# Layer 0 attention: the squares' sums are dealt out by a transfer, the key bias is a column of the keys, and rounding and queries change engines

## The chip, the cores and the metric

One Trainium2 chip (trn2), and the program runs on one of its cores. The metric is the device time of one execution in microseconds (us); less is better. Engines are TensorE (PE; PEld its weight loads), VectorE (DVE), ScalarE (ACT), GpSimd (POOL) and SyncE (SP), which issues nearly all DMAs.

## The reference

Two layers of gated cross attention with a feed-forward part behind each. The change lies in layer 0's attention, of which this is what matters (B = 4 batches, S = 256 tokens, 1601 context positions, H = 256, 8 key groups of 2 heads, head size D = 128):

```python
q  = ln(fp8_linear(ln_out, wq))  * qln_w  + qln_b      # per head, over D
k  = ln(fp8_linear(ln_out, wk))  * kln_w  + kln_b
qx = ln(fp8_linear(ln_out, wqx)) * qxln_w + qxln_b
kx = ln(einsum(cond, w_kv_x)[k]) * kxln_w + kxln_b
core = softmax(q  @ k.T  / sqrt(D)) @ v                # 256 own keys
xout = softmax(qx @ kx.T / sqrt(D)) @ vx               # 1601 context keys
cat  = concatenate([core, xout])
catq = fp8(bf16(clip(cat / smooth, -448, 448)))
x = x + tanh(g) * (catq @ wproj.T) * scale
```

## The kernel before

The program is written engine by engine: each of `sp_attention`, `pool_attention`, `dve_attention`, `act_attention` and `pe_attention` is one loop with its steps in an order chosen by hand, and semaphores join them. An iteration `it` is one pair of batch and key group (NGB = 32 of them). In iteration `it` the engines compute the attention of pair `it` (four query tiles `n = 4*it ... 4*it+3` of 128 rows) and prepare keys, values and queries of pair `it + 1`. During iterations 0 to 11 the weights of later groups are split into bf16 high and low parts as well.

Every product in fp32 quality is made of bf16 parts: a tensor has a high part and a low part (the remainder), and three products (`THREE`) are added. Keys and queries are `KK` and `QT`, values `VV`, probabilities `PB`, which DMA transposes turn into `PT`.

*Keys.* TensorE makes the unnormed keys of a pair in four blocks of PSUM (`keys`). ScalarE writes the high part (`keys_high`) times the norm's weight, and the squares `sq`; VectorE writes the low part (`keys_low`). The norm's factor of each key is not put into the keys: it multiplies the scores. For it TensorE sums the squares over D against a tile of ones (`squares`, 468 columns into each of four rows' groups), ScalarE copies the sums to `sqs` (`sums_out`), four transposes put them on partitions (`turn_squares`), VectorE copies them with epsilon to `ssc` [117 x 16] (`squares_out`), POOL raises them to the power -1/2 (`key_norm`, `rr`), TensorE transposes `rr` (`turn_norms`), ScalarE copies it to `rsr` (`norms_out`), and SP writes 16 rows of 468 bytes to DRAM (`row_out`) and reads them back as one row for all 128 partitions (`row_in`; its target is `x` for even and `rsb` for odd pairs).

*Scores.* `scores(n, half)` makes 1024 and then 577 + 256 columns. `scaled(n, piece)` on VectorE multiplies the scores by the row of factors, writes them to `S32` and takes the maximum (`mxp`, `mx`). `offset(n)` forms `nmx = c - (mx + c)`, where `c` is the bias of the keys times the query, which shifts all scores of a row alike. `c` comes from eight products with one column (`kb`, in `values(it, 3)`), which ScalarE copies from PSUM to `cb`. Then ScalarE takes exponentials, VectorE inverts the sums (`invert`), ScalarE writes the high probabilities (`p_hi`), VectorE the low ones (`p_lo`), and POOL both for the 256 own keys (`split_self`). SP transposes them (`turn_p`), and `times_v` multiplies by the values.

*Queries.* `turn_queries` leaves transposed normed queries in PSUM; ScalarE writes the high part `QT` from it (`query_high`), VectorE the full one `t32` (`query_full`), POOL the difference (`query_low`).

*Rounding to fp8.* VectorE divides, clips and takes the exponent bits `ye` (`exponents`); POOL makes the number `ym` from them (`magnitudes`: at least 2^-6, times 1.5 * 2^20) and adds and takes it away again (`add_magnitudes`, `take_magnitudes`). Then `project` multiplies with `wpb`, the split projection weights; `wpr` holds them as loaded.

*What sets the order.* SP issues one DMA after the other, so a wait holds everything behind it. The blocks of `SLOTS` take the three PSUM banks `pa`, `tb0`, `tb1` in turn; `wait_bank` waits until the block three slots before is read. A half of a score waits for the scaling of the same half of the score before:

```python
if n:
    e.wait_ge(s["mm"], 3 * (n - 1) + (1, 3)[half])
```

Of the kernel before, what the change touches and what calls it, by code (L numbers as in the profile page):

```python
# [13 lines left out]
P = 128  # L14
# [14 lines left out]
KC = SC + S  # L29
KTILES = KT + TB  # L30
# [12 lines left out]
ROUND_F8 = 1.5 * 2.0 ** 20  # L43
ROUND_INT = 1.5 * 2.0 ** 23
# [13 lines left out]
DCOLS = ["qln_w", "qln_b", "qxln_w", "qxln_b", "kln_w", "kln_b", "kxln_w", "kxln_b"]  # L58
# [14 lines left out]
pa_full k_sq k_lo sums_out ssq_out kr_pow rst_out v_hi v_lo st_done mv_done rs_pow nm_done normed  # L73
q_hi q_t32 q_lo pw_in pw_last pw_hi pw_lo acc_done
bank_full mm maxed negmax exp_s sum_read p_pad p_hi p_lo s_hi s_lo
# [28 lines left out]
def build(nc, A, out):  # L104
    m = Mem()
    whole = ExitStack()
    with whole:
# [5 lines left out]
        m.rs_d = nc.dram_tensor("rs_d", (2, SQN, SQW), F32, kind="Internal").ap()  # L113
# [9 lines left out]
def allocate(nc, m, whole):  # L123
# [15 lines left out]
    m.kb = sb(whole, "kb", [P, 2], BF16)  # L139
# [12 lines left out]
    with ExitStack() as attn:  # L152
# [7 lines left out]
        with ExitStack() as c:  # L160
            sb(c, "free_start", [P, BEFORE], BF16)
            m.wf = [sb(c, "wf0", [P, IC, WCOLS], F32), None]
            sb(c, "free_keys", [P, 2 * 2 * NQ * P + 2 * KC - 2 * IC * WCOLS], BF16)
# [17 lines left out]
        with ExitStack() as c:  # L181
            m.stage = [sb(c, f"stage{i}", [P, STAGE], BF16) for i in range(2)]
            m.wsb = sb(c, "wsb", [P, 2 * IC * WCOLS], BF16)
            m.sq = sb(c, "sq", [P, RSC], F32)
            m.sqs = sb(c, "sqs", [P, SQT * SQW], F32)
# [4 lines left out]
            kk[0] = sb(c, "KK0", [P, 2, KC], BF16)  # L190
            vv[0] = sb(c, "VV0", [P, 2, KTILES, D], BF16)
            sb(c, "free_mid", [P, 256], F32)
            qt[1] = sb(c, "QT1", [P, 2, 2, NQ * P], BF16)
            kk[1] = sb(c, "KK1", [P, 2, KC], BF16)
# [13 lines left out]
            m.ssc = sb(c, "ssc", [P, SQN], F32)  # L208
            m.rr = sb(c, "rr", [P, 32], F32)
            m.rsr = sb(c, "rsr", [32, P], F32)  # L210
            m.cb = [sb(c, f"cb{i}", [P, 2 * NQ], F32) for i in range(2)]
            m.mxp = [sb(c, f"mxp{i}", [P, 1], F32) for i in range(2)]
            m.mx = [sb(c, f"mx{i}", [P, 2], F32) for i in range(2)]
            m.mxc = [sb(c, f"mxc{i}", [P, 2], F32) for i in range(2)]
# [5 lines left out]
            m.ym = sb(c, "ym", [P, 512], F32)  # L220
# [6 lines left out]
        with ExitStack() as c:  # L227
# [14 lines left out]
            m.wg = sb(c, "wg", [P, IC, NE], F32)  # L242
            m.brow = sb(c, "brow", [P, NE], F32)
# [304 lines left out]
def pool_prologue(e, m, s):  # L548
# [9 lines left out]
    e.memset(m.rr[:, :], 0.0).then_inc(s["p_pad"], 1)  # L558
    e.memset(m.sq[:, KC:RSC], 0.0).then_inc(s["p_pad"], 1)
# [235 lines left out]
def pe_prologue(e, m, s):  # L795
# [8 lines left out]
         ("V2",), ("RS", "V3"), ("PR",))  # L804
ORDER = tuple(w for slot in SLOTS for w in slot)
SLOT = {w: n for n, slot in enumerate(SLOTS) for w in slot}
RS0 = 392
LAG = 3

PAIRS = 2 * G  # L810
# [77 lines left out]
def wait_bank(e, s, it, what):  # L888
# [6 lines left out]
    if SLOTS[at] == ("PR",) and 0 <= it < LAG:  # L895
        at -= 3
# [1993 lines left out]
```

## Time and profile before

| what | value |
|---|---|
| time, median of 3 runs (lowest to highest) | 1789.63 us (1786.24 to 1790.2) |
| span of the profiled execution | 1787.7 us |
| time of that execution around its span | not shown on the page |
| PE busy | 1631.5 us (91%) |
| DVE busy | 1474.9 us (83%) |
| ACT busy | 1386.3 us (78%) |
| POOL busy | 1367.9 us (77%) |
| DMA queue q1 | 602960 packets, 258.57 MB, 70.1% of 16 engines |

A profile is one execution. Busy times of the engines overlap, so an engine's share says how full it is and not what the end depends on; that is read from gaps, waits and the distance from start to start. Ends of matmuls are modelled: of matmuls the starts are read. Instructions of a group run on in the next row's time by some hundredths.

### The profile page before, as it was taken

The page shows a single profiled execution, that of the slowest core. Times are in us where ns is not written, and L with a number is a line of the kernel's source. Part 1 is how long each engine was busy: PE and PEld are TensorE (multiplying, and loading weights), DVE is VectorE, ACT ScalarE, POOL GpSimd, SP SyncE. Part 2 cuts the span into 40 slices and gives each one's busy share as a digit, 9 for nine tenths or more (in the row PEclk, how much of TensorE's full clock was granted, in tenths as well). Part 3 has the DMA queues.
Part 4 walks back from the last instruction along what each step waited for, and adds up shares of the span by engine and source line. Part 5 has one row for each costly group of instructions (what it writes and reads, how often), then busy time and mean ns, then how long its engine had stood idle before and what let it go on. Part 6 is the DMA issues. An engine that isn't in the chain of part 4 may idle for free. (4 is left out here: it accounts for less than half of the span.)

```text
span 1787.7 us, 44278 instructions
## 1 busy us (share of the span) xinstructions
PE 1631.5 (91%) x16245; PEld 1038.3 (58%) x16438; DVE 1474.9 (83%) x3476; ACT 1386.3 (78%) x2365; POOL 1367.9 (77%) x1171
## 2 busy tenths in 40 slices
PE   3389999999999999999999999997898999999997
PEld 1256776777767767777777777765454333333332
DVE  8889999999999989999999999998896765645422
ACT  4287887888878777887887888775234999999996
POOL 3557787887878888888888888887897998979500
PEclk8599999999999999999999999999899999999999
DMA  4268999999899979999999999998523222222100
GB/s 168 93 130 180 184 187 193 198 194 190 189 199 184 200 150 198 191 231 184 195 195 192 217 213 190 194 186 160 171 42 110 41 44 75 43 37 43 31 14 13
DMA packets 603176, 261.42 MB, mean 146 GB/s; under 512 B 568784, under 2 KB 575952, under 8 KB 601552
## 3 DMA queue, kind: packets, MB, share of 16 engines
q1 hardware_dynamic: 602960, 258.57, 70.1%
q8 instruction: 131, 2.15, 0.5%
q14 instruction: 85, 0.70, 0.1%
HBM read 99.15 MB, written 17.28 MB: 65 GB/s over the span
## 5 line engine op out<-in xcount | busy, mean ns | idle before, releaser
L1800 PE MATMUL pv<-PT,VV 128*128 128x256 bf16 (+1 forms) x2880 | 340.9, 275 | 9.2 <-DMA PT<-PB 9.2
L1780 PE MATMUL score<-KK,QT 128*128 128x512 bf16 (+2 forms) x1795 | 315.6, 318 | 32.6 <-DVE mxp L1249 24.3
L2370 POOL TENSOR_TENSOR l_rr<-l_rr,mhalf 128x32 f32<-128x32 f32 (+1 forms) x60 | 332.8, 5546 | 5.0
L1521 ACT ACTIVATE PB<-S,rsum 128x1024 bf16<-128x1024 f32 (+1 forms) x256 | 246.2, 988 | 105.3 <-DVE rsum L1281 101.1
L1800 PEld LDWEIGHTS pv<-PT,VV 128*128 128x128 bf16 (+1 forms) x2880 | 280.7, 99 | 76.4 <-issue 35.2
L1272 DVE SCALAR_TENSOR_TENSOR PB<-S,rsum,PB 128x1024 bf16<-128x1024 f32 (+1 forms) x256 | 318.7, 1246 | 2.7 <-ACT PB L1521 2.6
L1780 PEld LDWEIGHTS score<-KK,QT 128*128 128x128 bf16 x1920 | 159.9, 98 | 164.5 <-DVE mxp L1249 32.3
L1511 ACT ACTIVATE S<-S,nmx 128x1601 f32<-128x1601 f32 x128 | 209.7, 1638 | 28.3 <-DVE nmx L1263 27.8
L2636 ACT ACTIVATE P<-score 128x1024 f32<-128x1024 f32 x196 | 199.4, 1063 | 12.7 <-PE score L2728 6.0
L1076 POOL TENSOR_SCALAR S<-S,rsum 128x256 f32<-128x256 f32 x128 | 122.0, 954 | 86.1 <-DVE rsum L1281 86.1
L2748 PE MATMUL pv<-P,V 128*9 128x256 f32 (+1 forms) x2288 | 153.9, 384 | 3.8 <-DVE pv L2174 2.4
L1637 PE MATMUL tb<-stage,wsb 128*128 128x512 bf16 x767 | 150.7, 340 | 4.9 <-DVE stage L625 4.1
L1088 POOL TENSOR_SCALAR ym<-ye 128x512 f32<-128x512 bf16 x64 | 139.9, 2186 | 11.5 <-POOL catq L1104 5.4
L1059 POOL TENSOR_TENSOR rr<-ssc,mhalf 117x16 f32<-117x16 f32 x32 | 92.8, 2899 | 49.0 <-DVE ssc L1215 49.0
L1249 DVE CUSTOM_DVE_ANT_0 S<-score,x 128x1024 f32<-128x1024 f32 (+1 forms) x128 | 104.4, 816 | 7.0 <-PE score L1780 3.2
L1461 ACT ACTIVATE kn<-pa,a_nm,a_rs 128x128 f32<-128x128 f32 x256 | 96.0, 457 | 18.3 <-POOL a_nm L1041 18.3
L1249 DVE CUSTOM_DVE_ANT_0 S<-score,rsb 128x1024 f32<-128x1024 f32 (+1 forms) x128 | 104.4, 815 | 5.7 <-PE score L1780 1.9
L1637 PEld LDWEIGHTS tb<-stage,wsb 128*128 128x128 bf16 x768 | 67.3, 99 | 71.6 <-issue 10.6
L1689 PE MATMUL tb<-wsb,stage 128*128 128x128 bf16 x1536 | 98.1, 221 | 4.4 <-DVE KK L1161 4.4
L2728 PE MATMUL score<-QB,KT 32*128 32x256 bf16 (+1 forms) x1110 | 93.5, 275 | 7.0 <-ACT P L2636 4.7
L1430 ACT ACTIVATE KK<-tb,dcols 128x512 bf16<-128x512 f32 (+1 forms) x128 | 76.0, 593 | 28.6 <-PE tb L1637 27.9
L1689 PEld LDWEIGHTS tb<-wsb,stage 128*128 128x128 bf16 x1536 | 92.7, 99 | 8.4 <-DVE KK L1161 6.9
(275 smaller groups left out, 3686.7 us busy)
## 6 DMA issues: line engine op xcount, KB each, us to landing
x<-rs_d SPq DMA_DIRECT2D x16, 936.0 KB, 7.6
rsb<-rs_d SPq DMA_DIRECT2D x16, 936.0 KB, 6.0
wsb<-w_split SPq DMA_DIRECT2D x46, 256.0 KB, 4.7
wsb<-w_split SPq DMA_DIRECT2D x23, 512.0 KB, 5.2
wpr<-in_wprojT SPq DMA_DIRECT2D x23, 512.0 KB, 3.9
context_d<-stage SPq DMA_DIRECT2D x16, 400.2 KB, 3.7
l_ctx<-context_d SPq DMA_DIRECT2D x4, 1601.0 KB, 8.1
rawh<-in_w_all SPq DMA_DIRECT2D x12, 512.0 KB, 5.6
```

What stands on the lines that cost most here:

```text
L1088: e.tensor_scalar(m.ym[:, :], m.ye[:, :], 2.0 ** -6, ROUND_F8, ALU.max, ALU.mult).then_inc(s["y_mag"], 1)
L1249: e.tensor_tensor_reduce(m.S32[par][:, at:at + b - a], m.score[:, a:b], m.rsb[it % 2][:, key:key + b - a], 1.0, start, ALU.mult, ALU.max, ...
L1272: e.scalar_tensor_tensor(m.PB[n % 2][:, lo:lo + b - a], m.S32[n % 2][:, a:b], m.rsum[n % 2][:, 1:2], m.PB[n % 2][:, 2 * a:a + b], ALU.mult ...
L1511: e.activation(x, x, ACT.Exp, bias=m.nmx[par][:, 1:2], accum_out=m.sums[par][:, 1:2])
L1521: e.activation(m.PB[n % 2][:, 2 * a:a + b], m.S32[n % 2][:, a:b], ACT.Copy, scale=m.rsum[n % 2][:, 1:2]).then_inc(s["p_hi"], 1)
L1637: r = e.matmul(bank[:, 0:b - a], wk[:, w, ic, D:2 * D], ctx_op(m, it, part, ic, a, b), start=(n == 0), stop=(n == 5))
L1689: r = e.matmul(bank[:, h * D:(h + 1) * D], ctx_op(m, it, part, ic, t * P, (t + 1) * P), wv[:, w, ic, D:2 * D], start=(n == 0), stop=(n == 5))
L1780: i = e.matmul(m.score[:, at:at + b - a], qt[:, kind, qp, q * P:(q + 1) * P], kk[:, kp, a:b], start=(k == 0), stop=(k == 2))
L1800: i = e.matmul(m.pv[:, at:at + 256], vv[0:rows, v, t, :], m.PT[k % 2][0:rows, turned(c, a), :], start=(c == first and r == 0), stop=(c == ...
L2370: e.tensor_tensor(rr, rr, m.mhalf[0:rows, 0:NH1], ALU.pow).then_inc(s["l1_rr"], 1)
L2636: e.activation(pr[:, :], bank, ACT.Exp, scale=float(D1) ** -0.5).then_inc(s["l1_exp"], 1)
L2748: r = e.matmul(m.pv[j * R:j * R + VC, 0:S], m.V1[p][0:rows, t, 4 * hq + j, :], probabilities(m, n, j // 2)[0:rows, at:at + S], start=(t == ...
```

## The change

- The sums of squares (now 480 columns into each of four groups of rows) are copied by ScalarE with epsilon added, ahead of the probabilities' high part and the second query norm. SP deals them out: a transfer from the four rows of `sqs` to `ssc` [128 x 15] (`turn_sums`), issued between the transposes of tile `4*it` and of tile `4*it + 1`. `turn_squares`, `squares_out`, `turn_norms` and `norms_out` go. POOL's power works on 128 x 15 and comes behind `split_self(4*it + 1)`; `row_out` takes `rr` as it is, 128 rows of 60 bytes. `row_in` goes ahead of `load_projection`.
- The key bias is a column of its own behind each kind of keys (`KCOLS = KC + 2`), written by VectorE in the first two pairs only. So the scores have its product as one more column (66 and 257 columns where there were 65 and 256), and `offset` reads `c` from there in two operations. The eight products and `cb` go. As `offset` reads PSUM now, the second half of a score waits for the offset of the tile before.
- The number for rounding is made by VectorE from the exponent bits as integers (at least 0x3C80, plus 0x0A40) in bf16, two buffers; POOL's `magnitudes` goes.
- ScalarE writes the full fp32 query from PSUM, POOL casts it to the high part and takes the difference.
- POOL's operations of one step get a second one (times 1.0). `wg` and `brow` move to memory of the whole program, and `ssc`, `rr` and others change size.

```diff
+KCOLS = KC + 2
+LEAST_BITS, ROUND_BITS = 0x3C80, 0x0A40
+SQW = P * SQC // SQG
+BIAS = (SELF0 + S, SC)
...
+    def turn_sums(it):
+        e.wait_ge(s["sums_out"], it + 1)
+        if it:
+            e.wait_ge(s["kr_pow"], it)
+        e.dma_start(m.ssc[:, :], m.sqs[0:SQG * R:R, :].rearrange("j (r c) -> j r c", c=SQC)).then_inc(s["sums_in"], 16)
...
     def row_out(it):
-        e.wait_ge(s["rst_out"], it + 1)
+        e.wait_ge(s["kr_pow"], it + 1)
...
-        e.dma_start(m.rs_d[it % 2], m.rsr[0:SQN, 0:SQW]).then_inc(s["rs_row"], 16)
+        e.dma_start(m.rs_d[it % 2], m.rr[:, :]).then_inc(s["rs_row"], 16)
...
+        if it >= 0:
+            turn_sums(it + 1)
         turn_p(4 * it + 1, 0)
         row_out(it + 1)
+        row_in(it + 1)
         if it < NGB:
             load_projection(it - 1)
...
-        row_in(it + 1)
...
     def query_low(it, i):
+        e.tensor_copy(m.QT[it % 2][:, kind, 0, :], m.t32[:, :]).then_inc(s["q_hi"], 1)
+        e.wait_ge(s["q_hi"], c + 1)
         e.tensor_tensor(m.QT[it % 2][:, kind, 1, :], m.t32[:, :], m.QT[it % 2][:, kind, 0, :],
                         ALU.subtract).then_inc(s["q_lo"], 1)
...
-        e.tensor_scalar(m.ym[:, :], m.ye[:, :], 2.0 ** -6, ROUND_F8, ALU.max, ALU.mult).then_inc(s["y_mag"], 1)
...
     def offset(n):
-        e.wait_ge(s["v_hi"], 4 * it + 4)
-        e.tensor_tensor(m.mxc[par][:, :], m.mx[par][:, :], c, ALU.add).then_inc(s["maxed"], 1)
-        e.wait_ge(s["maxed"], n + 1)
...
-        e.tensor_tensor(m.nmx[par][:, :], c, m.mxc[par][:, :], ALU.subtract).then_inc(s["negmax"], 1)
+        for kind in range(2):
+            c, top = m.score[:, BIAS[kind]:BIAS[kind] + 1], m.mx[par][:, kind:kind + 1]
+            i = e.scalar_tensor_tensor(m.nmx[par][:, kind:kind + 1], top, c, c, ALU.add, ALU.subtract, reverse1=True)
+        i.then_inc(s["negmax"], 1)
...
     def exponents(k):
+        e.wait_ge(s["y_exp"], k + 1)
+        e.tensor_scalar(m.ym[k % 2][:, :].bitcast(I16), m.ye[:, :].bitcast(I16), LEAST_BITS, ROUND_BITS, ALU.max,
+                        ALU.add).then_inc(s["y_mag"], 1)
...
     def scores(n, half):
-        if n:
-            e.wait_ge(s["mm"], 3 * (n - 1) + (1, 3)[half])
+        if n and half == 0:
+            e.wait_ge(s["mm"], 3 * (n - 1) + 1)
+        elif n:
+            e.wait_ge(s["negmax"], n)
         parts = ((1, 0, 512, 0), (1, 512, 1024, 512)) if half == 0 else (
-            (1, 1024, 1536, 1024), (1, 1536, SC, 1536), (0, SC, KC, SELF0))
+            (1, 1024, 1536, 1024), (1, 1536, SC + 1, 1536), (0, SC + 1, KCOLS, SELF0))
```

How it moves instructions. TensorE, from the squares of pair 1 to its last value block, in iteration 0. Before (`sqs` are the copied sums, `rr` the norms, `kb` the bias):

```order
L1659 MATMUL tb<-sq,ones 32x468 x4
L1689 MATMUL tb<-wsb,stage1 128x128 x24
L1670 MATMUL pa<-ident,sqs 117x128 x4
L1780 MATMUL score<-KK0,QT0 128x512 x3
L1780 MATMUL score<-KK0,QT0 128x65 x3
L1780 MATMUL score<-KK0,QT0 128x256 x3
L1689 MATMUL tb<-wsb,stage1 128x128 x24
L1738 MATMUL tb<-ident,kn1 128x128 x4
L1689 MATMUL pa<-wsb,stage1 128x128 x24
L1747 MATMUL tb<-ident,rr 32x117
L1697 MATMUL tb<-wsb,stage1 128x128 x8
L1702 MATMUL tb<-kb,QT1 128x1 x8
```

With the change:

```order
L1628 MATMUL tb<-sq,ones 32x480 x4
L1647 MATMUL tb<-wsb,stage1 128x128 x24
L1727 MATMUL score<-KK0,QT0 128x512 x3
L1727 MATMUL score<-KK0,QT0 128x66 x3
L1727 MATMUL score<-KK0,QT0 128x257 x3
L1647 MATMUL tb<-wsb,stage1 128x128 x24
L1691 MATMUL tb<-ident,kn1 128x128 x4
L1647 MATMUL pa<-wsb,stage1 128x128 x24
L1655 MATMUL tb<-wsb,stage1 128x128 x8
```

The transposes of `sqs` and `rr` and the products with `kb` are gone, and the scores have a column more.

SP, from the first transposes of tile 4 to the second one of tile 5, in iteration 1 (`PB` are the probabilities, `x<-rs_d` the broadcast of the row of factors, `wpr` the projection weights). Before:

```order
L975 DMA_TRANSPOSE PT0<-PB0 128x14x128 [waits tv_done,s_lo,p_lo]
L975 DMA_TRANSPOSE PT0<-PB0 128x16x128 [waits tv_done,p_lo]
L975 DMA_TRANSPOSE PT0<-PB1 128x16x128 [waits tv_done,p_lo]
L947 DMA rs_d<-rsr 16x117 [waits rs_in0,rst_out]
L938 DMA wpr<-in_wprojT 128x1024
L960 DMA x<-rs_d 128x1872 [waits mm,rs_row]
L975 DMA_TRANSPOSE PT0<-PB1 128x14x128 [waits tv_done,s_lo,p_lo]
```

With the change:

```order
L976 DMA_TRANSPOSE PT0<-PB0 128x14x128 [waits tv_done,s_lo,p_lo]
L976 DMA_TRANSPOSE PT0<-PB0 128x16x128 [waits tv_done,p_lo]
L940 DMA ssc<-sqs 128x1x15 [waits kr_pow,sums_out]
L976 DMA_TRANSPOSE PT0<-PB1 128x16x128 [waits tv_done,p_lo]
L948 DMA rs_d<-rr 128x15 [waits rs_in0,kr_pow]
L961 DMA x<-rs_d 128x1872 [waits mm,rs_row]
L931 DMA wpr<-in_wprojT 128x1024
L976 DMA_TRANSPOSE PT0<-PB1 128x14x128 [waits tv_done,s_lo,p_lo]
```

The sums' transfer has come in behind two transposes, and the broadcast stands ahead of the projection weights.

VectorE, between the scaling of the second score piece and of the next tile, in iteration 1 (`acc` is the low part of weights being split here, `yq` the values to be rounded). Before:

```order
L1259 TENSOR_TENSOR mxc0<-mx0,cb1 128x2
L1263 TENSOR_TENSOR nmx0<-cb1,mxc0 128x2
L618 SCALAR_TENSOR_TENSOR acc<-rawh,win,acc 128x256 x2
L1205 TENSOR_SCALAR t32<-tb,dcols 128x512
L1272 SCALAR_TENSOR_TENSOR PB1<-S32_1,rsum1,PB1 128x640
L1174 TENSOR_TENSOR VV0<-pa,VV0 128x512
L1249 ISA S32_1,mxp1<-score,rsb1 128x1024
L1249 ISA mxp1 128x1
L1301 TENSOR_SCALAR yq1<-yq1 128x512
L1305 TENSOR_SCALAR ye<-yq1 128x512
L1281 RECIPROCAL rsum0<-sums0 128x2
```

With the change:

```order
L1243 SCALAR_TENSOR_TENSOR nmx0<-mx0,score 128x1 x2
L616 SCALAR_TENSOR_TENSOR acc<-rawh,win,acc 128x256 x2
L1253 SCALAR_TENSOR_TENSOR PB1<-S32_1,rsum1,PB1 128x640
L1177 TENSOR_TENSOR VV0<-pa,VV0 128x512
L1231 ISA S32_1,mxp1<-score,rsb1 128x1024
L1231 ISA mxp1 128x1
L1282 TENSOR_SCALAR yq1<-yq1 128x512
L1284 TENSOR_SCALAR ye<-yq1 128x512
L1287 TENSOR_SCALAR ym1<-ye 128x512
L1262 RECIPROCAL rsum0<-sums0 128x2
```

The offset has another form, the full query has left, and `ym` has come in behind `ye`.

## Rows read from the trace of the kernel before

**Rows 1.** Stretches of the span: busy us and count per engine, PEclk, DMA share, GB/s.

```profile
86.11:176.22 90.11, 81.19 (x671) 55.38 (x681) 78.29 (x203) 72.07 (x147) 56.26 (x66) 0.95 0.77 160
176.22:546.42 370.20, 351.16 (x3211) 258.38 (x3250) 353.11 (x851) 302.26 (x626) 295.07 (x316) 1.00 0.93 191
...
658.28:797.57 139.29, 138.45 (x1286) 103.31 (x1301) 130.55 (x320) 111.94 (x210) 115.81 (x120) 1.00 0.99 201
...
834.09:1183.32 349.23, 346.82 (x3211) 258.20 (x3250) 330.90 (x801) 283.47 (x525) 299.17 (x303) 1.00 1.02 199
```

**Rows 2.** Waits from 140 to 1240 us: total us, how many, longest.

```profile
PE score L1780 <- DVE mxp L1249: 24.3, 15, 3.6
```

**Rows 3.** Timeline of TensorE in a period that splits weights: start us, length us.

```profile
291.11 0.67 PE L1670 MATMUL pa<-ident,sqs 128*117 128x128 f32 x4
291.83 1.02 PE L1780 MATMUL score<-KK,QT 128*128 128x512 bf16 x8
...
294.46 1.50 PE L1689 MATMUL pa<-wsb,stage 128*128 128x128 bf16 x24
295.81 0.27 PE L1747 MATMUL tb<-ident,rr 117*32 117x117 f32 x1
295.91 0.61 PE L1697 MATMUL tb<-wsb,stage 128*128 128x128 bf16 x8
...
297.12 2.32 PE L1780 MATMUL score<-KK,QT 128*128 128x512 bf16 x14
...
311.45 1.47 PE L1780 MATMUL score<-KK,QT 128*128 128x512 bf16 x6 [1.82 <-DVE mxp L1249]
```

**Rows 4.** Timeline of VectorE in the same period.

```profile
297.37 0.80 DVE L1205 TENSOR_SCALAR t<-tb,dcols 128x512 f32<-128x512 f32 x1
...
301.13 0.29 DVE L1305 TENSOR_SCALAR ye<-yq 128x512 int16<-128x512 int16 x1
```

**Rows 5.** Timeline of TensorE, from the squares of one period to the next.

```profile
834.09 0.99 PE L1659 MATMUL tb<-sq,ones 128*32 128x468 f32 x8
...
857.06 1.47 PE L1780 MATMUL score<-KK,QT 128*128 128x512 bf16 x6
858.37 2.46 PE L1800 MATMUL pv<-PT,VV 128*128 128x256 bf16 x21
...
868.98 0.99 PE L1659 MATMUL tb<-sq,ones 128*32 128x468 f32 x8
```

**Rows 6.** Timeline of TensorE's squares and of SP's issues in a later period.

```profile
939.36 0.99 PE L1659 MATMUL tb<-sq,ones 128*32 128x468 f32 x8
...
941.35 5.03 SPq L975 DMA_TRANSPOSE PT<-PB  x2
...
950.54 1.70 SPq L938 DMA_DIRECT2D wpr<-in_wprojT  x1
952.93 0.32 SPq L960 DMA_DIRECT2D x<-rs_d  x1
```

**Rows 7.** DMA issues (at 950.17, 952.93, 953.35 and 412.7): KB, us to landing.

```profile
x<-rs_d SPq DMA_DIRECT2D x1, 936.0 KB, 7.6
...
rs_d<-rsr SPq DMA_DIRECT2D x1, 7.3 KB, 2.7
PT<-PB SPq DMA_TRANSPOSE x1, 8.9
...
rsb<-rs_d SPq DMA_DIRECT2D x1, 936.0 KB, 5.4
```

**Rows 8.** Groups by line and timeline rows: POOL's power, two equal VectorE operations, the start's rounding.

```profile
L1059 POOL TENSOR_TENSOR rr<-ssc,mhalf 117x16 f32<-117x16 f32 x32 | 92.8, 2899 | 49.0 <-DVE ssc L1215 49.0
...
938.63 1.25 DVE L1272 SCALAR_TENSOR_TENSOR PB<-S,rsum,PB 128x1024 bf16<-128x1024 f32 x1
...
955.48 2.37 DVE L1272 SCALAR_TENSOR_TENSOR PB<-S,rsum,PB 128x1024 bf16<-128x1024 f32 x1
...
65.97 3.31 DVE L634 TENSOR_SCALAR xq<-xq 128x1536 bf16<-128x1536 bf16 x1
```

More of the change, by code:

```diff
@@ L138, in allocate @@
     m.ones = sb(whole, "ones", [P, R], F32)
-    m.kb = sb(whole, "kb", [P, 2], BF16)
+    m.wg = sb(whole, "wg", [P, IC, NE], F32)
+    m.brow = sb(whole, "brow", [P, NE], F32)
     m.rsmc = sb(whole, "rsmc", [P, 2 * G * HPG], F32)
@@ L219, in allocate @@
             m.ye = sb(c, "ye", [P, 512], BF16)
-            m.ym = sb(c, "ym", [P, 512], F32)
+            m.ym = [sb(c, f"ym{i}", [P, 512], BF16) for i in range(2)]
             m.yt = sb(c, "yt", [P, 512], F32)
@@ L894, in wait_bank @@
         it, at = it - 1, at + len(SLOTS)
-    if SLOTS[at] == ("PR",) and 0 <= it < LAG:
+    if not SLOTS[at] or SLOTS[at] == ("PR",) and 0 <= it < LAG:
         at -= 3
@@ L1447, in values_high @@
         e.copy(flat(vv[:, 0, 12:14, :]), bank[:, 0:256])
-        if it >= 2:
-            e.wait_ge(s["negmax"], 4 * (it - 1))
-        e.copy(m.cb[it % 2][:, :], bank[:, 3 * D:3 * D + 2 * NQ])
         e.copy(vv[0:TAIL, 0, 14, :], bank[0:TAIL, 256:384]).then_inc(s["v_hi"], 1)
@@ L1480, in sums_out @@
         if it:
-            e.wait_ge(s["pa_full"], made(it - 1, "ST"))
-        e.copy(m.sqs[:, :], bank_of(m, "SS")[:, 0:SQT * SQW]).then_inc(s["sums_out"], 1)
-    def norms_out(it):
-        if not it < NGB:
-            return
-        e.wait_ge(s["pa_full"], made(it, "V3"))
-        if it:
-            e.wait_ge(s["rs_row"], 16 * it)
-        e.copy(m.rsr[0:SQN, 0:SQW], bank_of(m, "RS")[0:SQN, RS0:RS0 + SQW]).then_inc(s["rst_out"], 1)
+            e.wait_ge(s["sums_in"], 16 * it)
+        e.activation(m.sqs[:, :], bank_of(m, "SS")[:, 0:SQW], ACT.Copy, bias=D * EPS5).then_inc(s["sums_out"], 1)
     def projection_high(i):
@@ L1655, in squares @@
         if it == 0:
-            e.wait_ge(s["p_pad"], 2)
-        w = SQT * SQW
+            e.wait_ge(s["p_pad"], 1)
         for j in range(SQG):
-            r = e.matmul(bank[j * R:(j + 1) * R, 0:w], m.ones[:, :], m.sq[:, j * w:(j + 1) * w], start=True, stop=True,
-                         skip_group_check=True)
-        r.then_inc(s["pa_full"], 1)
-    def turn_squares(it):
-        if not it < NGB:
-            return
-        bank = bank_of(m, "ST")
-        wait_bank(e, s, it, "ST")
-        e.wait_ge(s["sums_out"], it + 1)
-        for t in range(SQT):
-            r = e.transpose(bank[0:SQW, t * P:(t + 1) * P], m.sqs[:, t * SQW:(t + 1) * SQW], m.ident[:, :])
+            r = e.matmul(bank[j * R:(j + 1) * R, 0:SQW], m.ones[:, :], m.sq[:, j * SQW:(j + 1) * SQW], start=True,
+                         stop=True, skip_group_check=True)
         r.then_inc(s["pa_full"], 1)
@@ L1698, in values @@
                              start=(n == 0), stop=(n == 3))
-            e.wait_ge(s["q_hi"], 2 * it + 2)
-            for kind, q in itertools.product(range(2), range(NQ)):
-                at = 3 * D + kind * NQ + q
-                e.matmul(bank[:, at:at + 1], m.QT[it % 2][:, kind, 0, q * P:(q + 1) * P], m.kb[:, kind:kind + 1],
-                         start=True, stop=True)
             for n, (ic, part, w) in enumerate(inner):
@@ L1739, in turn_queries @@
         r.then_inc(s["pa_full"], 1)
-    def turn_norms(it):
-        if not it < NGB:
-            return
-        bank = bank_of(m, "RS")
-        wait_bank(e, s, it, "RS")
-        e.wait_ge(s["kr_pow"], it + 1)
-        e.transpose(bank[0:R, RS0:RS0 + SQW], m.rr[0:SQW, :], m.ident[0:SQW, 0:SQW]).then_inc(s["pa_full"], 1)
     def project(i):
```

160 lines of the change are left out of this document (61 added, 99 removed).

## The prediction

> **What bounds the kernel now.** I read the stretches first. Layer 0's attention runs from about 86 to 1183 us, one period per pair of batch and key group. Where no weights are split, TensorE is busy 138.45 of 139.29 us in four periods and 346.82 of 349.23 us in ten, so 34.82 and 34.92 us a period; VectorE stands at 130.55 and 330.90 us, some 94%. In the ten periods that also split weights, a period is 37.02 us and VectorE is busy 353.11 of 370.20 us [rows 1]. So TensorE sets the pace in 18 periods (these 14 and four between them), and in the others VectorE holds it back. The waits say where: TensorE's scores waited 24.3 us for VectorE's scaling (mxp) in 15 waits [rows 2]. One of these is 1.82 us long, in front of the score that starts at 311.45 [rows 3].
>
> Since TensorE is dense, an instruction taken off it is worth its distance from start to start, as long as nothing else becomes late.
>
> **TensorE, removed.** The four transposes of the squares' sums: 291.11 to 291.83, 0.72 us. The transpose of the norms: 295.81 to 295.91, 0.10 us. The eight one-column bias products have no length of their own in the rows, since their weight loads run into their neighbours. From 295.91 to 297.12 pass 1.21 us for them and 14 value products; 24 such products take 294.46 to 295.81, 0.056 each, so the 14 take 0.79 and the eight 0.42 us. Sum 1.24 us a period [rows 3]. Added: 24 score columns and 48 sums' columns; the page has no row for a column, at the rate of the 128-column products (0.056 us) they are 0.03 us together. Net 1.2 us; the period can fall to 33.6 us.
>
> **VectorE.** It gives up two full-query products a period of 0.80 us each [rows 4] and the copy of the sums, and gains two `ym` operations. These have the form of `ye` (0.29 us, [rows 4]); I take 0.3 each, with 0.2 and 0.5 as ends, because two arithmetic steps may run slower than one AND. The offset shrinks from two dependent operations with a wait between them to two one-column ones without; no row prices the new form, I take 0.2 us less in all, between nothing and 0.4. The column of the key bias costs two operations in two periods, nothing. In a split period the path is a loop: TensorE's second value block ends, VectorE works without a gap up to the scaling that releases the score at 311.45 [rows 3]. On VectorE's side of the loop 0.80 of one full query and three times 0.2 fall away and 0.3 comes: 1.1 us. On TensorE's side the 0.72 us of transposes fall away. Sum 1.8 us, which is about the whole stall of 1.82, so 37.0 becomes 35.2 us.
>
> **ScalarE and POOL.** ScalarE writes the full query in fp32 where it wrote the bf16 one, the same length, and drops two small copies; its query is ready a VectorE operation earlier, so the bank is free sooner. POOL gives up two `ym` and takes two casts; it had idle time and has more. Both cost nothing on the path.
>
> **The sums' new way.** Now: transpose, VectorE, POOL's power, transpose, ScalarE, DRAM, broadcast. Then: ScalarE, a transfer on SP, the power, DRAM, broadcast, and this loop I must put into one period, counted from the squares' product. Two transposes of probabilities stand ahead of it on SP: the first is issued at 941.35, 2.0 us after the squares at 939.36, and as VectorE gets ahead of TensorE by up to 0.7 us I take 1.3; both issues last 5.0 us together, which stays [rows 6]. The sums go at 6.3. A small transfer just behind a transpose landed after 2.7 us [rows 7], so 9.0. The power took 2.90 us for 16 columns [rows 8], 2.7 for 15: 11.7. To DRAM 2.1 us, between half of that landing and the whole, as the queue is quieter then: 13.8, where the broadcast is issued. Before, it is issued at 952.93, 13.6 us after the squares [rows 6]. Alone it lands in 5.4 us [rows 7]: 19.2. Scaling takes 1.2 us, and TensorE wants it at 857.06 - 834.09 = 22.97 [rows 5], less 1.2, so 21.8: hidden, by 1.4 us.
>
> **What is late next.** The projection weights (`wpr`) are now issued behind the broadcast, and a transpose of probabilities behind both. Broadcast and weights together took 10.0 us from the issue at 950.54 to the landing at 960.53 [rows 6, 7], of which SP stood 2 us waiting for the row in DRAM, so 8: 21.8. The transpose behind landed 1.7 us later (953.35 plus 8.9): 23.5. TensorE's product wants it at 858.37 - 834.09 = 24.28 [rows 5], less 1.2, 23.1. So in the 13 periods that load these weights about 0.5 of the 1.2 us is given back, 0.7 stays; the five others keep 1.2.
>
> The row to DRAM is now 128 rows of 60 bytes, where it was 16 of 468, and the sums arrive as such rows too; nothing in the trace prices such short rows, and the bounds are nothing and, at the worst, another landing of 2.7 us. By the Trainium skill, page "DMA: Bandwidth & Descriptors", section on why a DMA increments its semaphore by 16, the number of engines must divide the slowest dimension of both sides. The sums' source has 4 rows, so by that rule four engines carry 32 pieces each; no row here shows what this costs. By it the sum would move towards the second rival.
>
> **Start and end.** In the first two periods I take 2 us each, for the reasons of a split period. At the start VectorE no longer does the full query in front of the rounding at 65.97, which lasted 3.31 us beside POOL's tensor operation [rows 8]; without it the rounding may come first. Between nothing and 4 us, I take 3. The last stage keeps its instructions; nothing.
>
> **Sum.** 13 x 0.7 + 5 x 1.2 = 15; split 10 x 1.8 = 18; first two periods 4; start 3: 40 us. The profiled execution spans 1787.7 us, the page shows no time around it, and the median is 1.9 above the span. From the median: 1750 us.
>
> **Rivals.** (a) The new wait for the offset. The second half of a score now waits for the maximum's offset and not only for the scaling, and in one of four an operation on probabilities stands between. Or VectorE does not gain what I say and TensorE's saved 1.2 us turns into waits for scaling. For: VectorE is at 94%. Against: it loses 1.1 us where it matters. Then some 20 of the 40 us stay: 1770. Chance 0.2.
>
> (b) Slower, through one mechanism: the sums' transfer and the row to DRAM land late, at SP, in every period. If the broadcast is issued at 17 and not 13.8, the transpose behind lands at 26.7 where weights are loaded; from TensorE's product to the next squares pass 868.98 - 858.37 = 10.6 [rows 5], so these 13 periods take 37.3, 2.4 us more than now, 31 us. The five others take 17 + 5.4 + 1.2 + 11.9 = 35.5, 0.7 more, 4 us. Of the split periods five load weights and lose 0.3 each, five save 1.5, together 6 us; start and first periods save perhaps 2. That gives 1817. It decides from an issue at about 16.0 on, where the same sum is nil. Against: a longer period lets VectorE's work, and so the first transpose, come earlier against the squares, which takes back part. Chance 0.08.
>
> (c) More than forecast. A probabilities operation on VectorE took 2.37 us at 955.48 beside POOL's work, 1.25 us is its length elsewhere [rows 8]. POOL loses the long `ym`. If VectorE then never holds TensorE, split periods fall to 33.6, 3.4 us each, and 16 us more are won, with some in the periods that load weights: 1730. Chance 0.14. The Trainium skill, page "SBUF — State Buffer", section "Who interferes with whom", says a VectorE operation with two SBUF inputs and a POOL operation that reads SBUF exclude each other; the trace agrees with 2.37 against 1.25 us. The same rule speaks against part of the change, as the new `ym` on VectorE can be held by POOL too.
>
> (d) No difference: a path through SP's queue was as long as TensorE's already. 0.04.
>
> **How the numbers follow.** The forecast has 0.54. About 0.2% (3.6 us) is what a measurement tells from no change. Faster takes the forecast, (a) and (c): 0.88; slower (b), 0.08; the same 0.04. The range leaves out the far halves of (a), (b) and (c): 1728 to 1778 us.
>
> **What would show it.** Right: no transposes of sums on TensorE; periods of 34.0 to 34.3 us with weights loaded and of 33.6 without, in split ones about 35.2 with the wait for scaling nearly gone; the broadcast issued about 14 us after the squares. Wrong: products waiting for the transposed probabilities, scores waiting for the offset, scaling waiting for the broadcast.

## The result and the profile after

1770.51 us is the median of 4 runs (1764.82 to 1772.7), against 1789.85 for the kernel before, run beside it. The ratio is 0.989, with a 95% interval of 0.9873 to 0.9907. So the change gains 19 us, not 40. A second measurement of the same two kernels, further on, gave 1765.9 us against 1789.53, a ratio of 0.9867 (0.9848 to 0.9886): 24 us. The two lie 4.6 us apart, so no difference of that size between kernels that were measured at different times is read as one below.

The page of the kernel after, its span and busy times:

```profile
span 1769.4 us, 43086 instructions
...
PE 1605.0 (91%) x15829; PEld 1008.5 (57%) x16022; DVE 1431.2 (81%) x3447; ACT 1376.7 (78%) x2301; POOL 1283.2 (73%) x1170
```

Every engine is less busy, VectorE by 44 us and POOL by 85. Stretches of the same work, cut at the starts of the squares (columns as in [rows 1]):

```profile
175.51:535.15 359.64, 341.87 (x3081) 248.94 (x3120) 332.14 (x840) 298.72 (x606) 270.55 (x316) 1.00 0.92 197
535.15:1172.69 637.54, 615.43 (x5546) 448.45 (x5617) 583.58 (x1423) 505.46 (x904) 495.24 (x544) 1.00 0.92 195
644.47:679.00 34.53, 34.13 (x310) 24.95 (x313) 32.16 (x80) 28.14 (x51) 27.30 (x31) 1.00 0.88 185
...
1033.11:1069.48 36.37, 34.40 (x310) 24.79 (x313) 32.67 (x81) 28.41 (x53) 27.74 (x31) 1.00 0.96 195
```

The ten split periods took 370.20 us before [rows 1] and take 359.64. The 18 behind them took 636.90 us (546.42 to 1183.32) and take 637.54: in this execution nothing came of what TensorE sheds. The profiled execution of the second measurement has 630.84 there and 356.92 in the split periods, so a stage of one execution is known to some 7 us. TensorE is no longer dense, 615.43 of 637.54 us. Single periods there lie between 34.06 and 38.79 us (the longest took 41.80 before), where before 34.82 repeated. Here are the waits for transfers in these 28 periods, and TensorE's wait for VectorE's scaling (us in total, times, longest):

```profile
POOL rr L1065 <- DMA ssc<-sqs: 89.9, 27, 7.0
...
ACT PB L1489 <- DMA PT<-PB: 16.0, 16, 2.9
...
PE pv L1747 <- DMA PT<-PB: 12.8, 20, 1.4
...
PE score L1727 <- DVE mxp L1231: 11.5, 18, 1.7
...
ACT wpb L1469 <- DMA wpr<-in_wprojT: 9.0, 8, 2.2
...
DVE S L1231 <- DMA rsb<-rs_d: 8.7, 6, 2.5
...
DVE S L1231 <- DMA x<-rs_d: 2.5, 2, 1.5
```

Products wait for transposed probabilities 20 times (twice before, 1.2 us), and scaling waits for the broadcast: two of the three wrong signs that the prediction names. Scores wait for scaling nearly as long, 11.5 us (before, 15.6 us in 11 waits). TensorE, SP and POOL in one period that loads projection weights, to set beside [rows 6]:

```profile
961.74 1.01 PE L1628 MATMUL tb<-sq,ones 128*32 128x480 f32 x8
...
963.95 5.31 SPq L976 DMA_TRANSPOSE PT<-PB  x2
969.35 0.58 SPq L940 DMA_DIRECT2D ssc<-sqs  x1
970.02 1.85 SPq L976 DMA_TRANSPOSE PT<-PB  x1
974.46 0.34 SPq L948 DMA_DIRECT2D rs_d<-rr  x1
977.47 0.32 SPq L961 DMA_DIRECT2D rsb<-rs_d  x1
977.84 0.42 SPq L931 DMA_DIRECT2D wpr<-in_wprojT  x1
...
971.52 2.91 POOL L1065 TENSOR_TENSOR rr<-ssc,mhalf 128x15 f32<-128x15 f32 x1 [2.88 <-DMA ssc<-sqs]
```

The sums go 7.6 us after the squares and the broadcast 15.7. Over the 31 periods the medians are: first transposes 1.8 us after the squares, sums 7.1, power 10.2, row 13.1, broadcast 15.2 (12.3 to 17.6). ScalarE has the sums ready at 1.7 us in the median. For over 5 us they lie there while SP issues two transposes of probabilities.

### The profile page after: what moved, and what is told of

It reads as the page before. It is cut to its first block and busy times, and to the rows that moved or that the text cites. A ratio compares the mean times of both kernels' runs of the same rounds, so it can differ in the third digit from the quotient of the medians.

```text
span 1769.4 us, 43086 instructions
## 1 busy us (share of the span) xinstructions
PE 1605.0 (91%) x15829; PEld 1008.5 (57%) x16022; DVE 1431.2 (81%) x3447; ACT 1376.7 (78%) x2301; POOL 1283.2 (73%) x1170
## 5 line engine op out<-in xcount | busy, mean ns | idle before, releaser
L2579 ACT ACTIVATE P<-score 128x1024 f32<-128x1024 f32 x196 | 199.1, 1060 | 13.1 <-PE score L2671 6.4
L1065 POOL TENSOR_TENSOR rr<-ssc,mhalf 128x15 f32<-128x15 f32 x32 | 91.4, 2856 | 100.2 <-DMA ssc<-sqs 100.2
L1082 POOL TENSOR_SCALAR S<-S,rsum 128x256 f32<-128x256 f32 x128 | 91.8, 717 | 79.4 <-DVE rsum L1262 69.0
L1040 POOL TENSOR_SCALAR a_nm<-a_mv 128x4 f32<-128x4 f32 x64 | 53.1, 829 | 77.9 <-DVE a_mv L1197 77.9
L1086 POOL TENSOR_TENSOR PB<-S,PB 128x256 bf16<-128x256 f32 x128 | 93.7, 732 | 10.9
```

Source lines behind the costliest of these rows:

```text
L2579: e.activation(pr[:, :], bank, ACT.Exp, scale=float(D1) ** -0.5).then_inc(s["l1_exp"], 1)
```

## Experiments on the sums' way

Theory 1: the new way lands late, at SP, and gives back what TensorE sheds. Theory 2: the way is hidden, and other terms failed.

**Old way.** All of the change but the sums' way, which goes through `turn_squares`, `squares_out`, `turn_norms` and `norms_out` again. With it come back the late copy of the sums, the power ahead of `split_self(4*it + 1)` and the weights ahead of the broadcast:

```diff
+        turn_squares(it + 1)
         scores(4 * it + 2, 1)
...
+        turn_norms(it + 1)
         values(it + 1, 3)
```

> The changed kernel (1770.5 us) with the sums of squares on their old way: transposes of sums and norms on TensorE, VectorE's copy to ssc, row of 16 x 468 bytes, sums copied late. Key bias as a column, ym on VectorE, queries by ScalarE and the two-step POOL operations stay. Theory 1 (the new way lands late and gives back what TensorE saves): this kernel is no slower than the changed one, 1765 to 1772 us. Theory 2 (the new way is hidden and worth what TensorE sheds, 0.8 to 1.0 us in some 30 periods, and the forecast failed by VectorE's part): 1792 to 1800 us, slower than the kernel before it would be without the other parts' gain, at least 1785.

1759.38 us against 1788.0, 0.9835 (0.9816 to 0.9854). The rest of the change alone is worth 29 us, and the part that sheds most on TensorE takes something away again: 11 us by the first measurement of the whole, whose interval lies clear of this one, and 7 by the second, whose interval touches it. Its ten split periods take 350.98 us, 19.2 less than before, and its regular ones 34.62 us.

**Row free.** `turn_sums` and `row_out` act for pair 0 only, and every later pair is scaled by pair 0's factors. This kernel leaves out what makes the row right, and serves only to time it:

```diff
...
-        e.wait_ge(s["rs_row"], 16 * (it + 1))
+        e.wait_ge(s["rs_row"], 16)
...
```

> The changed kernel with the sums' way cut open: only pair 0 is dealt out, raised and written to DRAM; all later pairs read that row again, so the transfer of the sums and the row to DRAM fall away and the broadcast waits for nothing but its buffer. Their norm factors are those of pair 0. POOL still takes the power, ScalarE still copies the sums. Theory 1: the lateness costs 10 to 20 us, so 1750 to 1760 us, with the waits for the transposed probabilities, the weights and the broadcast gone. Theory 2: within 3 us of the changed kernel's 1770.5.

1736.7 us, 0.9713 (0.9696 to 0.973): 29 us less than the changed kernel by its second measurement and 34 by its first, above what was expected. Two small transfers a period are gone here as well; that they are not what counts is shown by the kernel with the sums first, further on, which keeps them. TensorE's period is now 34.05 us.

**Order of weights and broadcast; load and sums.** In the one kernel `load_projection` stands ahead of `row_in` again, in the other `turn_sums` ahead of `load_weights(it + 2, 1)`:

```diff
         row_out(it + 1)
-        row_in(it + 1)
         if it < NGB:
             load_projection(it - 1)
...
+        row_in(it + 1)
```

```diff
         turn_p(4 * it, 0)
+        if it >= 0:
+            turn_sums(it + 1)
         if it + 2 < PAIRS:
             load_weights(it + 2, 1)
-        if it >= 0:
-            turn_sums(it + 1)
```

> The changed kernel with the projection weights issued ahead of the broadcast again, behind the row to DRAM. Theory 1 (what is late is the transpose of probabilities behind broadcast and weights, and ScalarE waiting for the weights): the broadcast lands some 0.5 us later, the weights 2 us earlier; within 2 us either way in all, 1768 to 1774. If the order itself was the loss: 1762 to 1767.

> The changed kernel with the sums' transfer issued ahead of the load of the query weights, which stood in front of it in those periods that load weights. Theory 1: the sums go up to 1 us earlier in the split periods where that load stands there, 1 to 4 us gained, 1766 to 1770. Theory 2: no difference, within 2 us of 1770.5.

1762.65 us (0.9829 to 0.9875 of before) and 1760.67 us (0.983 to 0.9861). The changed kernel's two intervals are 0.9873 to 0.9907 and 0.9848 to 0.9886; the first kernel overlaps both and the second the later one, so neither settles anything. The first lies in the range expected if the order itself was the loss, the second below both of its ranges. With the weights ahead, scaling's waits for the broadcast rise from 11 to 24 us and those for the transposes fall from 13 to 4: one late transfer for another.

> The changed kernel as it is, once more, as the measure for the three beside it. 1768 to 1772 us if it is stable.

1765.9 us, as told above, 2 us below the range that was expected.

**Sums first.** One step moved on SP:

```diff
+        if it >= 0:
+            turn_sums(it + 1)
         turn_p(4 * it, 1)
         turn_p(4 * it, 0)
...
-        if it >= 0:
-            turn_sums(it + 1)
         turn_p(4 * it + 1, 0)
```

> The changed kernel with the sums' transfer issued ahead of both transposes of tile 4*it's probabilities, not behind them. ScalarE has the sums at 1.7 us after the squares and the first transpose is issued at about 2, so the sums go some 5 us earlier and the transposes 0.6 later. Theory 1 (SP's two transposes in front of the sums are what makes the row late): the power starts 3 us earlier behind POOL's own work, broadcast and weights and the transpose behind them 2 to 3 us earlier; 1742 to 1755 us, close to the kernel whose row is free (1736.7). Rival (a transposed tile that comes 0.6 us later costs as much, or POOL holds the power): 1762 to 1772.

1736.78 us, 0.9718 (0.9698 to 0.9738): 29 us better than the changed kernel beside it, better than Theory 1 had it, and as good as the free row. Stretches, and one period of TensorE, SP and POOL:

```profile
172.72:520.82 348.10, 340.22 (x3082) 249.58 (x3121) 325.74 (x841) 300.53 (x606) 276.63 (x316) 1.00 0.95 205
520.82:1139.68 618.86, 609.96 (x5546) 450.93 (x5617) 549.96 (x1424) 505.24 (x906) 491.91 (x544) 1.00 0.97 201
661.45:695.50 34.05, 33.84 (x309) 25.06 (x312) 29.86 (x80) 27.11 (x52) 25.05 (x30) 1.00 0.95 204
```

```profile
935.33 1.01 PE L1628 MATMUL tb<-sq,ones 128*32 128x480 f32 x8
...
937.00 0.58 SPq L940 DMA_DIRECT2D ssc<-sqs  x1
937.70 6.98 SPq L976 DMA_TRANSPOSE PT<-PB  x3
944.76 1.03 SPq L948 DMA_DIRECT2D rs_d<-rr  x1
947.39 0.32 SPq L961 DMA_DIRECT2D rsb<-rs_d  x1
...
941.63 2.75 POOL L1065 TENSOR_TENSOR rr<-ssc,mhalf 128x15 f32<-128x15 f32 x1
```

The sums go at 1.7 us, POOL's power follows its own work without a wait, and the broadcast goes at 12.1 (median 12.7, against 15.2). 2.5 us there turn nearly every period behind the split ones into 34.05 us. Of the 89.9 us that POOL waited nothing is left, so POOL's other steps come earlier too.

**Sums by ScalarE.** `turn_sums` issued by ScalarE behind its own copy, and no longer by SP:

```diff
             sums_out(it + 1)
+            turn_sums(it + 1)
         p_hi(4 * it + 1, 0)
```

> The changed kernel with the sums' transfer issued by ScalarE right behind its own copy of the sums. It goes at about 2 us after the squares and SP's transposes keep their places, but ScalarE stands for the issue, some 0.6 us a period, beside work that had idle time before it. Theory 1: as the kernel with the sums first, or a little better, 1740 to 1755. Rival (ScalarE is held longer than its idle time, or the transfer stands behind the transposes in the DMA engines whichever queue issued it): 1760 or more.

1734.7 us, 0.9699 (0.9681 to 0.9717), not to be told from the sums first. It has the lowest median of all kernels here. By the Trainium skill, page "DMA: Bandwidth & Descriptors", section "Issuing engines are not separate DMA queues", a second issuing engine saves only the sequencer's time. The two results agree: what it saved was the place behind SP's 5.31 us of issuing, and a better place on SP saved as much.

## Experiments on the other parts

**Rounding number by POOL.** `magnitudes` back on POOL and `ym` in fp32, first on the changed kernel, then on the one with the sums first:

```diff
+        e.tensor_scalar(m.ym[:, :], m.ye[:, :], 2.0 ** -6, ROUND_F8, ALU.max, ALU.mult).then_inc(s["y_mag"], 1)
...
-        e.tensor_scalar(m.ym[k % 2][:, :].bitcast(I16), m.ye[:, :].bitcast(I16), LEAST_BITS, ROUND_BITS, ALU.max,
-                        ALU.add).then_inc(s["y_mag"], 1)
```

> The changed kernel with the number for rounding made by POOL again (in fp32, one buffer). VectorE gets back two times about 0.3 us a period; POOL gets its operation back and the chain to the projection in the last pairs becomes longer. If the move was worth what the forecast says (VectorE loses 0.3 us, POOL's time is free): 2 to 4 us faster in the periods that split weights. If it is what shortened the end of the attention by 7 us and took POOL's port from VectorE: 3 to 8 us slower.

> The kernel with the sums first (1736.8 us), with the number for rounding made by POOL again, as it was tried on the changed kernel, where it cost 50 us. Theory A (POOL's 2.1 us operation hurts because it and everything behind it stand behind a power that waits for late sums): with early sums it costs little, 1737 to 1750. Theory B (POOL is then simply too full, 4.3 us a period more beside the casts, whatever the sums do, and query norms come late): 1770 to 1790.

1815.95 us against 1789.53 (1.0158, 1.0134 to 1.0182), 50 us worse than the changed kernel, far outside what was expected, and 1756.99 (0.9824, 0.981 to 0.9837), 20 worse than the sums first. Neither theory is whole: some 30 of the 50 us need a power that waits for late sums, 20 remain with early ones. TensorE's waits say through what (first the changed kernel with POOL's number, then the sums first with it; in the 28 periods):

```profile
PE pa L1698 <- ACT kn L1444: 44.5, 26, 3.1
```

```profile
PE pa L1698 <- ACT kn L1444: 15.0, 14, 3.1
```

`kn` are the normed queries, which ScalarE makes when POOL has their factors (`a_nm`); for these ScalarE waited 61.6 and 44.1 us. TensorE's same wait was 6.0 us in the changed kernel and does not occur with the sums first. So POOL, with some 4 us more to do in a period, has the query norms late, as Theory B had it, and that is most of the 20 us. VectorE's probabilities are longer besides (sums first, then with POOL's number; us in all, mean ns):

```profile
L1253 DVE SCALAR_TENSOR_TENSOR PB<-S,rsum,PB 128x1024 bf16<-128x1024 f32 x232 | 268.5, 1157 | 0.5 <-ACT PB L1489 0.4
```

```profile
L1261 DVE SCALAR_TENSOR_TENSOR PB<-S,rsum,PB 128x640 bf16<-128x640 f32 x230 | 310.1, 1348 | 0.0
```

The same operations (both widths are in either group) take 0.19 us more each, eight a period: VectorE lost 1.5 us a period, more than the two `ym` of 0.30 us cost it here. It was not beside POOL's `ym` itself that they grew. Those of 1024 columns that began while it ran took 1.26 us (29 of them), those that began beside `yt`, POOL's sum of two tensors, 1.77 (26); the longer `ym` moves such operations to other places beside VectorE's. The page "SBUF — State Buffer" of the Trainium skill, section "Who interferes with whom", has a VectorE operation with two SBUF inputs contend with any POOL operation that reads SBUF, and the prediction weighed that section against the change. The trace agrees for `yt`, and does not show it for `ym`.

**Queries by VectorE.** On the kernel with the sums first, `query_high` and `query_full` as before:

```diff
-        e.tensor_copy(m.QT[it % 2][:, kind, 0, :], m.t32[:, :]).then_inc(s["q_hi"], 1)
...
+        query_full(it + 1, 0)
         if it == -1:
             dve_context_low(e, m, s, 1, 1)
```

> The kernel with the sums first, with the full queries written by VectorE again and the high ones by ScalarE, POOL's casts gone. The forecast's term: VectorE gets 0.80 us twice a period. In periods paced by TensorE (34.05 us) nothing, in those that split weights 0.8 to 1.6 us each: 1745 to 1752. Rival (VectorE has slack now, and POOL loses its 0.7 us casts, whose place is in front of the probabilities of the own keys): 1732 to 1739.

1736.85 us, 0.9718 (0.9704 to 0.9731): no difference. VectorE gets 0.80 us twice a period and POOL loses its two casts of 0.61 us; once the sums are early, the two together cost nothing. They were not tried apart.

**Bias column, alone and undone.** Alone on the kernel before; and undone on the kernel with the sums first, which puts back what the first takes out:

```diff
-                e.matmul(bank[:, at:at + 1], m.QT[it % 2][:, kind, 0, q * P:(q + 1) * P], m.kb[:, kind:kind + 1],
-                         start=True, stop=True)
...
+        elif n:
+            e.wait_ge(s["negmax"], n)
```

> The kernel before, with the key bias as a column of the keys alone: no one-column products, no copy of them, the offset in two operations from PSUM, and the second half of a score waiting for it. The forecast's term was 0.42 us a period on TensorE, 13 us over all. By the periods seen since (34.82 us before; 34.62 with everything but the sums' way) it is 0.20 us in some 18 periods, 4 us, and a little in the split ones by the shorter offset: 1780 to 1786. If the new wait for the offset costs: 1790 or more.

> The kernel with the sums first (1736.8 us), with the key bias by eight one-column products again, copied by ScalarE, and the offset from there in two dependent operations. If the column is worth what TensorE's periods show (0.20 us a period): 1741 to 1748. If the column's loss of 21 us on the kernel before is its own (the second half of a score waits for the offset): 1715 to 1732. If that loss came from POOL's being late there, which is gone here: the first.

1808.99 us, 1.0115 (1.0101 to 1.0129), and 1849.28 us, 1.0345 (1.0326 to 1.0364). The second lies far outside all that was expected; the first is in the range of a costly wait for the offset, but that wait is not in its trace. Of the 112 us that the second loses, 61 have a clear cause, TensorE's one-column products waiting for the high queries, which now come from POOL:

```profile
PE tb L1661 <- POOL QT L1056: 60.7, 26, 6.1
```

So with the products kept, the queries' move is costly; the column's own price can't be read from this kernel. For that the queries would have to go back too, which was not tried. Alone, its periods behind the split ones take about 36.1 us where 34.82 stood, though TensorE has less to do. Its waits (174 to 1175 us):

```profile
PE score L1776 <- DVE mxp L1252: 18.6, 12, 2.2
PE pa L1721 <- DVE t L1208: 8.0, 13, 0.6
PE pa L1732 <- ACT kn L1460: 7.2, 16, 2.8
```

The offset is not among them. The late ones are the full query on VectorE (`t`) and the query norm (`kn`), which ScalarE gets from POOL. VectorE's scaling now waits for POOL's split of the own probabilities, which it never did before:

```profile
DVE S L1252 <- POOL PB L1078: 10.8, 17, 0.7
```

That points to POOL being late, but no run tests it, and why it is later with the column is open.

**POOL's second step.** Undone on the fastest kernel, and alone on the kernel before. The scaling of the own probabilities is shown; two small operations on `a_nm` and `a_rs` change with it:

```diff
-        e.tensor_scalar(p, p, m.rsum[n % 2][:, 0:1], 1.0, ALU.mult, ALU.mult).then_inc(s["s_hi"], 1)
+        e.tensor_scalar(p, p, m.rsum[n % 2][:, 0:1], None, ALU.mult).then_inc(s["s_hi"], 1)
```

> The kernel whose sums' transfer ScalarE issues (1734.7 us), with POOL's one-step operations as before (no second step times 1.0). POOL's scaling of the own probabilities took 0.95 us on average before and 0.76 with two steps. If that is the form and not the neighbours, POOL gets 0.2 us four times a period, and has the time: within 2 us, 1733 to 1738. If POOL's time counts in the split periods: 1738 to 1745.

> The kernel before, with nothing but the second step (times 1.0) in POOL's operations. The scaling of the own probabilities took 0.93 us in one step in all its 111 instances and 0.48 in two; four a period are 1.8 us less on POOL. If POOL's lateness in the kernel before is part of what holds the split periods and the projection at the end: 8 to 20 us faster, 1770 to 1781. If POOL only matters once the casts are on it: within 3 us of 1788.

1755.84 us, 0.9818 (0.9805 to 0.9832), 21 us worse, where 11 at most were expected; and 1774.82 against 1785.3, 0.9935 (0.9921 to 0.995), 10 us better than before with nothing else changed. The scaling of the own probabilities, by line, in the kernel before, with the step alone, and in the fastest kernel without it:

```profile
L1076 POOL TENSOR_SCALAR S<-S,rsum 128x256 f32<-128x256 f32 x111 | 103.0, 928 | 56.8 <-DVE rsum L1281 56.8
```

```profile
L1076 POOL TENSOR_SCALAR S<-S,rsum 128x256 f32<-128x256 f32 x112 | 54.2, 484 | 75.5 <-DVE rsum L1281 69.9
```

```profile
L1080 POOL TENSOR_SCALAR S<-S,rsum 128x256 f32<-128x256 f32 x114 | 111.7, 980 | 79.6 <-DVE rsum L1260 79.6
```

Left alone, the operation with two steps takes half the time. In the two kernels of these lines without the step, no instance is shorter than 0.9 us; with the step alone nearly all are at 0.48. But its place counts as well. In the changed kernel, which has the step, 88 of 125 took under 0.6 us and the others up to 1.7, and the mean of those from 175 to 1175 us is 0.73:

```profile
L1082 POOL TENSOR_SCALAR S<-S,rsum 128x256 f32<-128x256 f32 x112 | 81.4, 727 | 51.6 <-DVE rsum L1262 46.0
```

Why one step takes longer than two is open.

**Rounding number by VectorE, alone** on the kernel before.

> The kernel before, with the number for rounding by VectorE alone: POOL loses two operations of 2.2 us a period, VectorE gains two of 0.3 to 0.5. By POOL's time, as above: 10 to 20 us faster, 1768 to 1778, of which some 5 lie behind the last squares. By the forecast's terms (VectorE is the bound in the split periods, POOL costs nothing): 3 to 8 us slower, 1791 to 1796.

1787.34 us against 1785.3, 1.0008 (0.9998 to 1.0018): no difference, and neither expectation. The split periods stay (371.18 us); what lies behind the last squares is 4.0 us shorter, the periods between 2.3 longer.

## Why the prediction was wrong

The direction and the range held; the forecast's 40 us came out as 19, and as 24 in the second measurement. The stages, from squares to squares in one profiled execution of each, us:

| stage | before | after | after, second | sums first | forecast |
|---|---|---|---|---|---|
| start to squares of pair 1 | 103.1 | 102.8 | 103.5 | 103.4 | -3 |
| first two periods | 73.1 | 72.7 | 74.2 | 69.4 | -4 |
| ten split periods | 370.2 | 359.6 | 356.9 | 348.1 | -18 |
| 18 periods behind them | 636.9 | 637.5 | 630.8 | 618.9 | -15 |
| rest | 604.4 | 596.7 | 597.6 | 595.1 | 0 |
| span | 1787.7 | 1769.4 | 1763.0 | 1734.8 | -40 |

**The sums' new way: the step that failed.** The step is the sum up to "13.8, where the broadcast is issued", which left the new way hidden or nearly so. The broadcast went at 15.2 in the median, and at 14.8 in the second execution. Its parts: first transposes 1.8 and not 1.3; sums 7.1 and not 6.3; power 10.2 and not 9.0; row 13.1 and not 11.7; broadcast, 2.1 later, as forecast. The first four steps were 0.2 to 0.5 short each, all in one direction. The allowance of 0.7 for VectorE getting ahead was too large (the first transposes went at 2.0 in the median before, at 1.8 after), and the power took 2.87 on average and not 2.7; the others were priced from single rows, and the medians are longer.

Put into the forecast's own working, 1.4 us later makes 24.9 where TensorE wants the transpose at 23.1. A period with weights then loses 0.6 instead of keeping 0.7, the others still keep their 1.2. The trace has 15 periods with weights among the 18, where the prediction counted 13 and five others. So its working gives 5 us more than before in place of 15 less; measured were 0.6 more and, in the second execution, 6 less. The working has the direction, and its size is not confirmed.

Nor was the transpose the only thing that became late. In these 18 periods TensorE waited 7.3 us for transposed probabilities, 4.2 for scaling, 3.4 for values that VectorE had not read yet and 3.3 for normed queries, 18.2 in all; with the sums first it waited 5.2. The periods took 18.7 us longer than with the sums first. So the mechanism of rival (b) acted, weaker than (b) priced it, together with the waits for scaling of rival (a), whose total of 1770 us came out. The new waits for the offset that (a) named first are small: 2.1 us in all, behind the last squares. The other miss lies deeper: the prediction took the two transposes ahead of the sums as given. Moving the sums past them gave 29 us, and taking the row away altogether gave no more.

**TensorE's 1.2 us a period (1.24 less what was added) were 0.77** (34.82 to 34.05), so the forecast 33.6 us never occurred, with weights or without. Of it 0.20 are the bias products and 0.57 the transposes, as the kernel with the old way (34.62) tells. TensorE in a period before and in one after:

```profile
696.33 1.50 PE L1689 MATMUL tb<-wsb,stage 128*128 128x128 bf16 x24
697.67 0.65 PE L1670 MATMUL pa<-ident,sqs 128*117 128x128 f32 x4
698.37 1.02 PE L1780 MATMUL score<-KK,QT 128*128 128x512 bf16 x8
...
702.46 0.61 PE L1697 MATMUL tb<-wsb,stage 128*128 128x128 bf16 x8
702.90 0.34 PE L1702 MATMUL tb<-kb,QT 128*128 128x1 bf16 x8
703.11 0.50 PE L1705 MATMUL tb<-wsb,stage 128*65 128x128 bf16 x6
703.66 0.60 PE L1780 MATMUL score<-KK,QT 128*128 128x512 bf16 x2
```

```profile
647.72 1.50 PE L1647 MATMUL tb<-wsb,stage 128*128 128x128 bf16 x24
649.28 1.02 PE L1727 MATMUL score<-KK,QT 128*128 128x512 bf16 x8
...
653.26 0.61 PE L1655 MATMUL tb<-wsb,stage 128*128 128x128 bf16 x8
...
654.26 1.92 PE L1727 MATMUL score<-KK,QT 128*128 128x512 bf16 x9
```

24 value products and the transposes lasted 2.04 us; the products alone, with a score behind them, 1.56, though with other work behind them they last 1.34. So the four transposes were worth 0.48, not their distance of 0.72. In the same way the 14 value products take 1.00 us in front of a score, not 0.79, which leaves 0.20 of 1.20 for the bias products, not 0.42. The trace had this price: from their start at 702.90 to the next start pass 0.21 us, where the prediction took them to have no length of their own. A distance from start to start holds the change to the next kind of work, which stays when the instruction goes.

**VectorE and the split periods.** 35.2 us was right for the change without the new way (350.98 / 10 = 35.1), 35.96 came out with it, 34.8 with the sums first. But its reason is not borne out: 0.8 us of the 1.1 on VectorE was the full query, and giving that back, together with POOL's casts, costs nothing with the sums early (346.6 us for the ten, against 348.1). POOL's second step, which the prediction did not price at all, is worth 13.4 us of the split periods in the fastest kernel (345.73 with it, 359.09 without) and 7.6 alone on the kernel before (362.55). How much of the 18 is VectorE's, how much POOL's, in the changed kernel itself, was not tried. `ym` took 0.47 us on average in the changed kernel (0.30 with the sums first), inside its bounds.

**Start.** VectorE's rounding did come first and was short, but the next operation took the time:

```profile
65.87 0.55 DVE L632 TENSOR_SCALAR xq<-xq 128x1536 bf16<-128x1536 bf16 x1
66.46 3.66 DVE L634 TENSOR_SCALAR ex<-xq 128x1536 int16<-128x1536 int16 x1
```

```profile
65.96 3.75 POOL L515 TENSOR_TENSOR xq<-y,mag 128x1536 bf16<-128x1536 f32 x1
```

3.31 us fell to 0.55 [rows 8] and 1.39 rose to 3.66: whichever of the two runs beside POOL's tensor operation is long. Of the 3 us, 0.3 came in one execution and nothing in the other.

**The rest, forecast at nothing,** gave 7.7 us. The attention's last iterations prepare no new pair, and what holds TensorE there are VectorE and POOL. Before, its waits from 1183 to 1300 us held 2.9 us for POOL's projection weights (`tb<-wpb`) and 7.3 for transposed probabilities; after, none and 4.5. `ym` alone shortens this stage by 4.0 us, the second step alone by 2.9, in one execution each.

**The first two periods** gave 0.4 of 4 us in one execution and took 1.1 us more in the other, with the sums late; they gave 3.8 with the sums first, 3.0 with the sums by ScalarE.

## What to carry to other kernels

Where a change replaces work on an engine by a transfer, look at what the issuing queue does at the moment the data are ready, and put the transfer ahead of it: here that place was worth 29 us, and the whole change 19 to 24. When a chain has to fit into a period, add its measured medians, not its shortest rows, and ask what a miss of 1 us does. Price an instruction to be removed by the same sequence without it, not by its distance to the next start, and count small form changes on an engine with slack: slack in the sum isn't slack in the order.

## What the runs showed of the hardware

POOL's multiplication of 128 x 256 fp32 by a value per partition took 0.93 us on average in one step in the kernel before, with no instance under 0.9, and 0.48 with a second multiplication by 1.0, where nothing held it; in the changed kernel the mean was 0.73. A small transfer behind two transposes on the same queue had to wait for the 5.31 us that issuing them took. With more work on POOL, VectorE's probabilities took 1.35 us on average instead of 1.16, longer beside POOL's sum of two tensors (1.77) and not beside its operation on one (1.26). At the start, a hold by POOL that no longer met one operation (3.31 to 0.55) fell on the next (1.39 to 3.66). 24 products of 128 columns took 1.34 us ahead of like work and 1.56 ahead of a score.
